# Score tiles of four heads with 32 queries each, in a fused attention and ternary feed-forward kernel on Trainium2

## The reference

```python
xn = layernorm(x)                                   # x: 4 x 1024 x 512
c_Q = rms_norm(xn @ Wq_down, q_norm_w)              # 192
q_nop = (c_Q @ Wq_up)                               # 16 heads x 128
q_pe  = rope(c_Q @ Wq_pe)                           # 16 heads x 64
c_KV = rms_norm(xn @ Wkv_down, kv_norm_w)           # 128
k_nop, v = split(c_KV @ Wkv_up, 2)                  # 8 heads x 128 each
k_pe = rope(rms_norm(xn @ Wk_pe, k_pe_norm_w))      # 64, for all heads
scores = (q_nop . k_nop + q_pe . k_pe) * 192 ** -0.5, causal mask
y = softmax(scores) @ v @ Wo
x_q = ternary(xn, 0.33, 0.5); w = ternary(weight, 0.2, 0.6) + rram_variation
out = x + y + x_q @ w.T
```

## Time and profile before

| | |
|---|---|
| median of three runs | 1688.98 us |
| the profiled execution's own time | 1687.28 us |
| its span | 1685.5 us |
| granted TensorE clock, mean | 0.993 |
| TensorE, VectorE, ScalarE, GpSimd busy | 97%, 78%, 66%, 35% |

### The profile page before, as it was taken

How to read it: one execution, slowest core, us unless ns; L and a number is a source line. 1 busy time by engine, 2 the same in 40 slices (tenths; PEclk the granted TensorE clock), 3 DMA queues, 4 the chain that set the end, 5 groups by cost and what they waited for, 6 DMA issues and landing times.

```text
span 1685.5 us, 33931 instructions
## 1 busy us (share of the span) xinstructions
PE 1636.6 (97%) x11532; PEld 915.8 (54%) x11532; DVE 1311.4 (78%) x3369; ACT 1117.6 (66%) x2464; POOL 597.6 (35%) x1080
## 2 busy tenths in 40 slices
PE   4789999999999999999999999999999999999999
PEld 3555555555555556555554555555555555655544
DVE  6888878768788788778878787876878878877765
ACT  5777767567676676657667676766767667666663
POOL 3333334333343333433333333433334333343330
PEclk8899999999999999999999999999999999999999
DMA  9336777758768678876858877766876867777776
GB/s 261 85 72 118 127 131 126 132 109 143 137 127 148 114 133 133 144 136 102 144 102 157 144 127 133 129 128 109 145 134 129 148 112 134 135 140 131 130 135 124
DMA packets 780264, 221.25 MB, mean 131 GB/s; under 512 B 766968, under 2 KB 769402, under 8 KB 779770
## 3 DMA queue, kind: packets, MB, share of 16 engines
q1 hardware_dynamic: 769392, 195.41, 66.5%
q10 hardware_dynamic: 9162, 17.37, 3.5%
q0 software_dynamic: 1536, 6.29, 1.1%
HBM read 19.76 MB, written 8.39 MB: 17 GB/s over the span
## 4 chain that ended last, share of the span: by engine, by line
PE 85%; DVE 5%; issue 4%; ACT 3%; DMA 2%; POOL 1%; SPq 0%; DVEq 0%; ACTq 0%; POOLq 0%
PE bank L718 6%; PE bank L720 6%; PE bank L719 6%; PE bank L721 6%; PE bank L816 6%; PE bank L818 6%; PE bank L817 6%; PE bank L763 5%; PE bank L764 5%; PE bank L765 5%; PE bank L731 4%; PE bank L484 2%; PE bank L485 2%; PE bank L518 1%; PE bank L523 1%
## 5 line engine op out<-in xcount | busy, mean ns | idle before, releaser
L1105 ACT ACTIVATE P<-P,nm 128x256 f32<-128x256 f32 (+15 forms) x512 | 381.9, 746 | 411.9 <-DVE nm L1509 411.2
L1509 DVE CUSTOM_DVE_ANT_0 P<-bank,mask,neg 128x256 f32<-128x256 f32 (+15 forms) x512 | 383.1, 784 | 244.3 <-PE bank L731 237.4
L1758 POOL TENSOR_SCALAR sn<-sm 128x1 f32<-128x1 f32 x512 | 208.3, 407 | 887.8 <-ACT P L1105 877.0
L1100 ACT ACTIVATE F<-P,rc 128x256 f16<-128x256 f32 (+15 forms) x512 | 365.2, 741 | 100.2 <-DVE rc L1517 61.9
L1523 DVE SCALAR_TENSOR_TENSOR F<-P,rc,F 128x256 f16<-128x256 f32 (+15 forms) x512 | 402.4, 798 | 2.8 <-ACT F L1100 2.4
L718 PE MATMUL bank<-K,Q 128*128 128x512 f16 (+7 forms) x760 | 241.8, 319 | 0.0
L720 PE MATMUL bank<-K,Q 128*128 128x512 f16 (+7 forms) x760 | 241.7, 319 | 0.0
L721 PE MATMUL bank<-K,QP 128*128 128x512 f16 (+7 forms) x760 | 241.7, 319 | 0.0
L719 PE MATMUL bank<-K,Q 128*128 128x512 f16 (+7 forms) x760 | 241.7, 319 | 0.0
L816 PE MATMUL bank<-WO,YH 128*128 128x512 f16 x512 | 194.3, 379 | 5.0 <-DVE YL L1529 4.7
L817 PE MATMUL bank<-WO,YH 128*128 128x512 f16 x512 | 194.0, 379 | 0.0
(11 more groups left out here) (226 smaller groups left out, 3222.6 us busy)
## 6 DMA issues: line engine op xcount, KB each, us to landing
out<-X ACTq DMA_DIRECT2D x31, 256.0 KB, 2.8
X<-in_x ACTq DMA_DIRECT2D x28, 256.0 KB, 4.2
FT<-F SPq DMA_TRANSPOSE x348, 4.2
wo<-in_Wo POOLq DMA_DIRECT2D x4, 1024.0 KB, 7.0
V<-CC SPq DMA_DIRECT2D x64, 32.0 KB, 3.0
QP<-QS SPq DMA_TRANSPOSE x128, 2.8
X<-in_x SPq DMA_DIRECT2D x4, 256.0 KB, 8.2
kv<-in_Wkv_up POOLq DMA_DIRECT2D x1, 1024.0 KB, 11.6
```

The source lines that it names most:

```text
L1100: return e.eng.activation(dst, src, ACT.Copy, scale=scale)
L1105: e.eng.activation(m.P[:, u % 4, 0:w], m.P[:, u % 4, 0:w], ACT.Exp, bias=m.nm[:, u % 8:u % 8 + 1], scale=-1.0, accum_out=m.sm[:, u % 8:u % ...
L1509: e.eng.tensor_tensor_reduce(out=m.P[:, u % 4, 0:w], in0=m.pS[u % 2][:, off:off + w], in1=m.mask[:, end - w:end], scale=m.neg[:, :], scala ...
```

## The change

A score tile now has all four heads of a group with 32 queries each. `row_block` says which 32 queries tile u has (0, 2, 1, 3 for the four tiles), and `columns` cuts 96, 32, 64 and 0 keys off the last block, in all groups. The mask is a 32 x 32 triangle for each head. The queries Q are stored by row block, so the stationary operand is one contiguous block of 128, and rows of x, keys, values and output lie in natural order: keys are turned straight into K, `keep_keys` and the buffer KT go, the values need one DMA in place of two.

The rotated queries come out of the DMA transpose by head, into a new buffer QT; a new VectorE instruction (`rotated_rows`) copies them into QP by row block. It stands in the second half of step n for group n + 3, and the scores wait for its semaphore qp. The high and low parts of the rotated queries are written by two instructions of 64 partitions each in place of one. What a score tile leaves out of F and the transposes read all the same is zeroed by GpSimd (`zero_gap`), which waits until the slot of F is free; the transposes wait for it (semaphore gap).

```diff
-def side(u):
-    return u % 4 // 2
+def row_block(u):
+    return 2 * (u % 2) + u % 4 // 2
...
-    return blocks_wide(u) - (64 if side(u) == 0 and not whole(u // 4) else 0)
+    return blocks_wide(u) - 96 + 32 * row_block(u)
...
+def gap_end(u):
+    if whole(u // 4):
+        return blocks_wide(u)
+    return columns(u) + (32 if row_block(u) % 2 == 0 else 0)
...
 def query_weights(m, n, h):
-    a, g = divmod(h, 2)
-    Q, heads = m.Q[:, n % 4, :, :], slice(2 * g, 2 * g + 2)
-    return [x[:, heads, :].rearrange("p h q -> p (h q)")[:, a::2] for x in (Q[:, 0:4, :], Q[:, 4:8, :], m.QP[:, n % 2, :, :])]
+    r = row_block(h)
+    return m.Q[:, n % 4, r, :], m.Q[:, n % 4, 4 + r, :], m.QP[:, n % 2, r, :]
...
     def pair(n, p):
...
-        e.wait_ge(s.q_in[n % 2], 16 * (n // 2 + 1))
-        e.wait_ge(s.k_at, n // NG + 1)
+        e.wait_ge(s.qp, n + 1)
+        e.wait_ge(s.k_in, 16 * (n // NG + 1))
...
     def rotated_hi(self, n):
...
-        e.eng.activation(rotated_parts(m, n)[0], m.R1.rearrange("p (g h) d -> p g h d", g=2), ACT.Copy).then_inc(s.ph, 1)
+        for a in range(2):
+            op = e.eng.activation(rotated_parts(m, n, a)[0], m.R1[64 * a:64 * a + 64, :, :], ACT.Copy)
+        op.then_inc(s.ph, 1)
...
+    def rotated_rows(self, n):
+        e, m, s = self.e, self.m, self.s
+        e.wait_ge(s.q_in[n % 2], 16 * (n // 2 + 1))
+        if n >= 2:
+            e.wait_ge(s.s, 4 * (n - 1))
+        e.eng.tensor_copy(m.QP[:, n % 2, :, :].rearrange("p r (h k) -> p r h k", k=32),
+                          m.QT[:, n % 2, :, :].rearrange("p h (r k) -> p r h k", k=32)).then_inc(s.qp, 1)
...
             if t + LEAD - 1 < T and (g, p) == ((0, 1) if t else (1, 0)):
                 tiles.parts_lo(t + LEAD - 1)
+            if p and n + AHEAD + 1 < N:
+                queries.rotated_rows(n + AHEAD + 1)
...
     def rotated_lo(self, n):
...
-        e.eng.tensor_tensor(lo, m.R1.rearrange("p (g h) d -> p g h d", g=2), hi, ALU.subtract).then_inc(s.pl, 1)
+        for a in range(2):
+            hi, lo = rotated_parts(m, n, a)
+            op = e.eng.tensor_tensor(lo, m.R1[64 * a:64 * a + 64, :, :], hi, ALU.subtract)
+        op.then_inc(s.pl, 1)
+        e.wait_ge(s.pl, n + 1)
...
+    def zero_gap(u):
+        slot, z, at = parts_place(u)
+        w, lo, end = columns(u), blocks_wide(u), gap_end(u)
+        if end == w:
+            return
+        if z >= FSLOTS:
+            e.wait_ge(s.ft_in[slot], 16 * (z // FSLOTS))
+        both = m.F[:, slot, at:at + 2 * lo].rearrange("p (x c) -> p x c", x=2)
+        e.eng.memset(both[:, :, w:end], 0.0).then_inc(s.gap, 1)
...
             if u < 4 * N:
                 scale_sum(u)
+                zero_gap(u)
                 scale_sum(u + 1)
+                zero_gap(u + 1)
...
-        e.eng.dma_start_transpose(out=m.KT[:, :, :],
+        e.eng.dma_start_transpose(out=m.K[:, :, at * 128:at * 128 + 128],
                                   in_=m.CC[:, 1, :, :].rearrange("p a n -> p (a n)")).then_inc(s.k_in, 16)
-        for a in range(2):
-            e.eng.dma_start(m.V[64 * a:64 * a + 64, at, :, :], m.CC[a::2, 1, :, 0:128]).then_inc(s.v_in, 16)
+        e.eng.dma_start(m.V[:, at, :, :], m.CC[:, 1, :, 0:128]).then_inc(s.v_in, 16)
...
-            e.wait_ge(s.s, 4 * (n - 1))
-        e.eng.dma_start_transpose(out=m.QP[:, n % 2, :, :], in_=m.QS[:, n % 2, :]).then_inc(s.q_in[n % 2], 16)
+            e.wait_ge(s.qp, n - 1)
+        e.eng.dma_start_transpose(out=m.QT[:, n % 2, :, :], in_=m.QS[:, n % 2, :]).then_inc(s.q_in[n % 2], 16)
```

More of the change, by code:

```diff
@@ L132, in columns, with gaps_before @@
 def columns(u):
-    return blocks_wide(u) - (64 if side(u) == 0 and not whole(u // 4) else 0)
-def mask_end(u):
-    return 1088 if side(u) == 0 and whole(u // 4) else 1024
+    return blocks_wide(u) - 96 + 32 * row_block(u)
[3 more added lines that the diff above has]
+    return columns(u) + (32 if row_block(u) % 2 == 0 else 0)
+def gaps_before(u):
+    return sum(gap_end(v) > columns(v) for v in range(u))
 def score_cuts(u):
@@ L253, in __init__ @@
         self.QP = own("QP", [128, 2, 4, 128], F16)
+        self.QT = own("QT", [128, 2, 4, 128], F16)
         self.QS = own("QS", [128, 2, 512], F16)
@@ L715, in pair @@
             e.wait_ge(s.mk, u - 1)
+            off, cuts = score_cuts(u)
             for lo, hi in cuts:
@@ L726, in pair @@
         if halved(n, p):
-            for lo, hi in cuts:
+            for c in range(len(cuts)):
                 for h, top in ((2 * p, 0), (2 * p + 1, 64)):
+                    off, cuts = score_cuts(4 * n + h)
+                    lo, hi = cuts[c]
                     o, keys = m.pS[h % 2][:, off + lo:off + hi], slice(base + lo, base + hi)
@@ L1119, in values_hi @@
             e.wait_ge(s.c, n - 1)
-        copy(placed(m.YH[:, n % 2, :]), natural(m.pY[n % 2])).then_inc(s.yh, 1)
+        copy(by_rows(m.YH[:, n % 2, :]), by_heads(m.pY[n % 2])).then_inc(s.yh, 1)
     def last_values_hi(p):
@@ L1125, in last_values_hi @@
         e.wait_ge(s.c, N - 2)
-        copy(placed(m.YH[:, (N - 1) % 2, 256 * p:256 * p + 256]), natural(m.pY[(N - 1 + p) % 2][:, 0:256])).then_inc(s.yh, 1)
+        copy(by_rows(m.YH[:, (N - 1) % 2, 256 * p:256 * p + 256]), by_heads(m.pY[(N - 1 + p) % 2][:, 0:256])).then_inc(s.yh, 1)
     def load_x(t):
@@ L1145, in store_half @@
         at = slice(256 * k, 256 * k + 256)
-        e.eng.dma_start(rows(out, T - 1)[:, :, at], m.X[:, (T - 1) % XSLOTS, at]).then_inc(s.st_o, 16)
+        e.eng.dma_start(rows(out, T - 1)[:, at], m.X[:, (T - 1) % XSLOTS, at]).then_inc(s.st_o, 16)
     def outputs_out(o):
@@ L1496, in vector_prologue @@
     queries.queries_lo(3)
+    queries.rotated_rows(0)
+    queries.rotated_rows(1)
 def vector_attention(e, m, s, tiles, queries):
     def maximum(u):
-        w, end = columns(u), mask_end(u)
+        w = columns(u)
         off, _ = score_cuts(u)
@@ L1508, in maximum @@
             e.wait_ge(s.ex, u - 7)
-        e.eng.tensor_tensor_reduce(out=m.P[:, u % 4, 0:w], in0=m.pS[u % 2][:, off:off + w], in1=m.mask[:, end - w:end],
+        e.eng.tensor_tensor_reduce(out=m.P[:, u % 4, 0:w], in0=m.pS[u % 2][:, off:off + w], in1=m.mask[:, 1024 - w:1024],
                                    scale=m.neg[:, :], scalar=3.0e38, op0=ALU.add, op1=ALU.min,
@@ L1582, in vector_attention @@
     outputs_lo(15)
+    queries.rotated_rows(2)
     for n in range(N):
@@ L1773, in gpsimd_attention @@
                 else:
+                    e.wait_ge(s.sm, u + 2)
+                    e.wait_ge(s.gap, gaps_before(u + 2))
                     queries.rotated_lo(n + 2 * AHEAD)
@@ L1781, in gpsimd_attention @@
                 tiles.x_lo(t + LEAD)
-            if (g, p) == (3, 1) and t + LEAD - 1 < T:
-                tiles.keep_keys(t + LEAD - 1)
 class SyncTiles:
@@ L1882, in turn_probabilities @@
         e.wait_ge(s.fl, u + 1)
+        if gaps_before(u + 1):
+            e.wait_ge(s.gap, gaps_before(u + 1))
         if n == N - 1:
```

125 lines of the change are left out of this document (55 added, 70 removed).

## The result

The changed kernel takes 2023.53 us (median of four runs, 2021.81 to 2026.07), the kernel before, run beside it, 1689.0 us. The ratio is 1.1986, interval 1.1973 to 1.2: slower by a fifth. The forecast was 2004 us, in a range of 1880 to 2105.

The account below looks back on a forecast made before the run. TensorE's stream was taken as the bound; 1687.3 - 15.7 (columns) + 217 (lateness) + 50 (copy) + 19 (ScalarE) - 8 (maximum) + 54 (clock) = 2004 us, range 1880 to 2105.

Parts of the forecast that it names:

- TensorE's columns: Narrower score tiles take 37,344 columns off TensorE's matmuls at 0.42 ns each: 15.7 us less.
- The lateness read off the old trace: TensorE's scores wait for the copy as long as VectorE runs behind at its place in the queue: 217 us.
- the copy: VectorE's 128 x 512 f16 copy QT to QP, taken as 0.45 us, at 118 places: 50 us, between 15 and 83.
- By kind of place: Lateness per place: narrow 2.04 us (62), first wide 2.03 (16), ahead of narrow 4.33 (9), other wide 0.43 (27).
- the nine places where VectorE was early: Last step of a wide tile with a narrow one next: VectorE 0.42 us early, so no wait.
- That the stalls do not heal: VectorE's lateness stems from each step itself, not carried over, so each step pays anew.
- the 0.73 that was named as a sign of being wrong: Sign: the prediction is wrong about VectorE's copy if it takes more than 0.73 us or waits for its DMA.
- ScalarE's second instruction: Second instruction for the rotated queries' high part delays the queries by 0.31 us, 61 times: 19 us.
- the narrower maximum: VectorE's maximum of the third tile is 64 columns narrower, 0.07 us at 118 places: 8 us back.
- The clock: TensorE's clock halves after one stall in three, some 42 drops at 1.3 us: 54 us, the least certain term.
- The rival in which the clock falls after every stall: TensorE's clock drops at all 118 stalls, 153 us instead of 54: 2103 us, chance 0.12.
- GpSimd's work, hidden: Second low part (100 us) and 268 gap memsets (40 us) covered by GpSimd's idle time; busy near 720 us.

Follow-up runs that it names:

- before_with_wait: The kernel before the change, plus a VectorE copy of 448 numbers to an unread place, which the scores wait for: 1983.25 us, ratio 1.1746.
- no_copy: The changed kernel without rotated_rows: TensorE reads QT itself and waits for its DMA; rotated scores are of other queries: 1693.71 us, ratio 1.0036.
- no_copy_one_scalar_part: The changed kernel without rotated_rows, ScalarE making its rotated-query part in one instruction, GpSimd keeping two of 64 partitions: 1676.89 us, ratio 0.9929.
- filled_stalls: The changed kernel with 1010 useless 512-column matmuls put ahead of TensorE's waits for the copy: 1948.61 us, ratio 1.1541.
- no_copy_no_gaps: The changed kernel without rotated_rows and without zeroing the gaps after the first eight groups: 1694.06 us, ratio 1.0025.
- no_copy_one_part: The changed kernel without rotated_rows, high and low rotated-query parts each made by one instruction of 128 partitions: 1678.3 us, ratio 0.9933.

## Why the prediction was right, step by step

- **TensorE's columns: 15.7 us off, measured 11.5.** The count of columns is that of the two width rules, and the price per column is in the rows: a second cut of 160 columns takes 0.07 us (810.00 to the next start 810.07) where one of 192 took 0.09. The saving is partly met by other waits. Which they are I did not separate.
- **The lateness read off the old trace, and the copy: 217 + 50 + 19 - 8 = 278 us, measured 267.1 in 107 waits.** This is the step that decided, and its mechanism held. The same lateness can be read off the old trace at each of the 107 places where TensorE came to wait, as the end of the VectorE instruction ahead of the copy's place less the start of the group's scores. It adds up to 238 us, all of it positive. The remaining 29 us are 0.27 us a place, about one copy.
- **By kind of place** the stalls of the changed trace are 159 us at the narrow places with the first groups (forecast 62 x 2.46 + 4 x 0.42 + 8 = 162), 35 at 15 of the 16 first groups of wide tiles (39), 46 at the nine places ahead of a narrow tile (43), and 27 at the other steps of wide tiles (23). Of those 27 steps only 18 waited, 1.5 us each instead of 0.85; at the other nine, those right behind the longest stalls (groups 25, 33, 41 and so on), the copy was done 0.2 us before TensorE came. At the nine places where VectorE was early nothing waited, as forecast.
- **Part of the closeness is luck.** The lateness was read too low (217 against 238 us) and what comes on top of it too high (50 + 19 - 8 = 61 against 29). One narrow place, group 45, stood for all, but they waited between 1.2 and 4.0 us, and it was only their mean, 2.44, that agreed with the 2.46 taken; group 45 itself waited 1.77.
- **That the stalls do not heal** was argued from one stretch. It held in the main: before_with_wait has stalls at as many places with the old tiles, and the 238 us of lateness came back nearly in full. It did not hold for the nine groups right behind the longest stalls.
- **The copy: 0.45 us taken, 0.329 measured,** 0.287 where it stands behind the maxima. In the changed kernel 17 of the 128 copies took over 0.4 us, the longest 0.78, above the 0.73 that was named as a sign of being wrong; behind the maxima none took over 0.33. By the Trainium skill (VectorE: DVE Perf Modes, "Mode 4×_2P — both tricks at once") the copy was an estimated 0.30 us. These rows agree with it, and it was nearer than the middle of my bounds.
- **ScalarE's second instruction: 19 us taken, 16.8 measured** (no_copy less no_copy_one_scalar_part). VectorE's waits for the queries went from 61 to 94, so the count behind the term was too low and its price too high. The 8 us for the narrower maximum were not measured alone.
- **The clock: 54 us taken, 75 measured** with filled_stalls. The low stretches of the changed trace behind the prologue add up to 177 us. Half of that, 89 us, is work put off, and most of it was on the path. I had taken 42 drops; there were 44. That the count came out is luck, since nothing in the rows gave one stall in three. The price was too low: 75 / 44 = 1.7 us a drop instead of 1.3, since eight of the 44 low stretches lasted 6.8 us and not 3.4, and less of it was hidden than the quarter that I took. The rival in which the clock falls after every stall was wrong: 44 drops against 107 stalls. The Trainium skill (TensorE: Matmul & The Clock Gate, "HAM oscillation — how this bites in real kernels") tells of idling between tiles that lowers the clock of the matmuls behind it, and of a kernel in which every tile starts so. filled_stalls agrees with the first: without the idling the clock stayed at 0.993. The second did not come about here: 63 of 107 stalls had no drop.
- **GpSimd's work, hidden: right.** no_copy_no_gaps shows it for the memsets, no_copy_one_part against no_copy_one_scalar_part for the second low part; its busy time is 714.6 us, forecast 720.

The parts add up: 1688.7 - 11.5 + 16.8 = 1694.0 us, measured 1693.7 without the copy. From there 267 of stalls and 75 of clock would be 342 more, measured 330. The two heads of pages show where the 12 us went. TensorE's idle time grows from 65.7 us (1691.4 - 1625.7) to 313.0, by 247 and not 267: some 20 us of waits that no_copy has elsewhere were taken over by the stalls. Its busy time grows from 1625.7 to 1708.3 us, by 83, which is the lower clock, 8 us more than filled_stalls gave. 247 + 83 = 330.

The forecast of 2004 us was 20 low. Against these parts it started 1.4 us too low, took 4 us too many off for the columns, had 14 too many for what TensorE waits (278 against 247 + 17), and 29 too few for the clock (54 against 83). So its largest single error was the clock, and the stalls took half of that back.

## What to carry to other kernels

Before an instruction is put into the queue of an engine that is not the bound, ask who will wait for it, and read in the trace how far that engine runs behind the waiting one at this place: the lateness costs nothing while nobody waits and becomes a stall in full once somebody does. The price can be read off the old trace, at every place and not at one of a kind, as the end of the work ahead of the place less the start of the waiting instruction. A copy of 0.3 us cost 330 us at the end of a step and 4 us, hardly more than the noise, behind the maxima. It must not stand where its own DMA has not landed either: ahead of the maxima it waited 69.6 us for that.

## What the runs showed of the hardware

- Useless matmuls made a kernel faster: 1010 of them, 218 us of work in stalls, gave 75 us; the mean granted clock was 0.993 instead of 0.954. A stall of TensorE of 2.5 us was followed by 3.4 us at half the clock, while 63 of the 107 stalls, the longest of them 3.5 us, had no drop.
- These ScalarE and GpSimd instructions took nearly as long on 64 partitions as on 128: 407 against 400 ns on ScalarE, 690 against 766 on GpSimd (no_copy_one_part). Splitting one by partitions took ScalarE's busy time for it from 51.2 to 104.1 us and GpSimd's from 98.1 to 176.6.
- VectorE's 128 x 512 copy of f16 inside SBUF, in runs of 32 numbers, takes 0.287 to 0.329 us in the mean and 0.28 at its shortest; the low part of as many numbers out of PSUM takes 0.68 to 0.73.
